# Convolution copies routed through DRAM in five transfers a piece, and the first worker's local attention woven with the tail of the second worker's scan

## What is computed

```python
# L0_attn: Mamba-2 on the GRU's output g; then x = x + branch + g
zxbcdt = g @ W_in
xBC = silu(causal depthwise convolution, 16 taps, of zxbcdt[..., 256:640] + conv_b)   # 384 channels
# y: the scan over 128 positions with the states B, C and dt
y = rmsnorm(y * silu(z)) @ W_out
t = y / sqrt(1 + y * y);  out = t @ W_nl + b_nl + g

# L0_cond2: attention to three neighbours and one conditioning key, 16 heads of 64
q, k = x @ WQ_w + WQ_b, x @ WK_w + WK_b;  ak, av = cond @ WK_w + WK_b, cond @ WV_w + WV_b
K = [ak, k[t-1], k[t], k[t+1]];  V = [av, k[t-1], k[t], k[t+1]]
att = softmax(q . K / 8) . V;  out = att @ WO_w + WO_b
```

## Time and profile before

| what | value |
|---|---|
| median of 3 executions (range) | 2227.7 us (2224.23 to 2228.19) |
| the profiled execution's own time | 2227.43 us |
| its span in the profile | 2225.7 us |
| mean granted TensorE clock | 0.951 of full speed |
| busy: PE / DVE / ACT / POOL | 1960.3 / 1593.2 / 1006.9 / 466.7 us |
| GRU ends, convolution and scan start | about 234 us |
| worker 0's / worker 1's Mamba ends | 606 / 649 us |
| attention ends | 1034 us |

### The profile page before, as it was taken

How to read it: one execution, slowest core, us unless ns; L and a number is a source line. 1 busy time by engine, 2 the same in 40 slices (tenths; PEclk the granted TensorE clock), 3 DMA queues, 4 the chain that set the end, 5 groups by cost and what they waited for, 6 DMA issues and landing times.

```text
span 2225.7 us, 63875 instructions
## 1 busy us (share of the span) xinstructions
PE 1960.3 (88%) x26197; PEld 1227.9 (55%) x26273; DVE 1593.2 (72%) x3661; ACT 1006.9 (45%) x2843; POOL 466.7 (21%) x816
## 2 busy tenths in 40 slices
PE   8989688888778989887899999967999789999998
PEld 5555233333353434434577767655666456677776
DVE  3444557777647787876988888726989578888887
ACT  3333347666622222122555555433554445555554
POOL 2221000000002343434012122254331111112100
PEclk9999789999969899997999999978999999999999
DMA  3000344332000000002211111016552211111111
GB/s 66 4 4 4 74 99 87 71 85 53 30 24 0 1 1 1 1 1 62 76 45 43 45 43 45 25 38 127 110 100 54 67 40 45 45 45 45 42 57 37
DMA packets 133228, 102.42 MB, mean 46 GB/s; under 512 B 23532, under 2 KB 114244, under 8 KB 131364
## 3 DMA queue, kind: packets, MB, share of 16 engines
q1 hardware_dynamic: 129352, 96.04, 17.8%
q10 hardware_dynamic: 3584, 2.30, 0.3%
HBM read 60.24 MB, written 11.82 MB: 32 GB/s over the span
## 4 chain that ended last, share of the span: by engine, by line
PE 47%; DVE 24%; ACT 12%; issue 9%; SPq 3%; DMA 2%; ACTq 1%; POOL 1%; another core or an unknown queue 0%; DVEq 0%; POOLq 0%
PE B L85 46%; DVE work L2251 4%; ACT catt L103 4%; DVE work L107 4%; DVE hr L2215 3%; DVE work L2259 3%; SPq L897 2%; ACT hr L103 2%; ACT ltc L103 2%; ACT work L103 2%; DVE work L1627 1%; DVE gzh L107 1%; ACT ghh L103 1%; ACTq L2538 1%; DVE lth L107 1%
## 5 line engine op out<-in xcount | busy, mean ns | idle before, releaser
L85 PE MATMUL B<-gr,wres 128*128 128x512 f32 x1248 | 352.9, 411 | 15.8 <-DVE work L2259 9.4
L103 ACT ACTIVATE work<-B 128x512 f32<-128x512 f32 (+6 forms) x462 | 236.3, 528 | 143.8 <-PE B L85 99.4
L2301 POOL COPY G<-lh 128x32 f32<-128x32 f32 x256 | 148.3, 579 | 679.9 <-DVE lh L107 679.9
L85 PEld LDWEIGHTS B<-gr,wres 128*128 128x128 f32 x1248 | 214.1, 189 | 82.6 <-DVE work L2259 26.8
L103 ACT ACTIVATE hr<-work 128x512 fp32r<-128x512 f32 x272 | 172.9, 636 | 147.8 <-DVE work L2259 77.8
L2215 DVE TENSOR_TENSOR hr<-work,hr 128x512 fp32r<-128x512 f32 x272 | 186.5, 686 | 8.1 <-ACT hr L103 6.6
L2251 DVE TENSOR_TENSOR work<-work 128x512 f32<-128x512 f32 x256 | 178.6, 698 | 14.7 <-ACT work L103 7.2
L85 PE MATMUL B<-hr,wres 128*128 128x512 f32 x624 | 178.0, 394 | 1.0 <-DVE hr L2215 1.0
L103 ACT ACTIVATE lth<-B 128x96 f32<-128x96 f32 (+1 forms) x512 | 86.7, 222 | 185.9 <-PE B L85 185.8
L85 PEld LDWEIGHTS B<-lh,lw 128*32 128x32 f32 x8128 | 88.5, 112 | 112.8 <-issue 58.6
L85 PE MATMUL B<-lh,lw 128*32 128x32 f32 x8128 | 116.7, 199 | 25.1 <-DVE lh L107 24.3
(11 more groups left out here) (270 smaller groups left out, 3850.2 us busy)
## 6 DMA issues: line engine op xcount, KB each, us to landing
work<-wdr SPq DMA_DIRECT2D x128, 256.0 KB, 3.1
spare<-work SPq DMA_DIRECT2D x288, 65.0 KB
scr<-catt SPq DMA_DIRECT2D x144, 64.0 KB, 2.8
spare<-spare SPq DMA_DIRECT2D x96, 65.0 KB
work<-scr SPq DMA_DIRECT2D x16, 384.0 KB
work<-scr SPq DMA_DIRECT2D x16, 192.0 KB
catt<-in_L_ffn_ew SPq DMA_DIRECT2D x24, 128.0 KB, 2.4
work<-scr SPq DMA_DIRECT2D x16, 128.0 KB
```

The source lines that it names most:

```text
L85: return e.matmul(out, lhsT, rhs, start=start, stop=stop, skip_group_check=True)
L103: return e.activation(out, in_, func, bias=bias, scale=scale)
L2301: e.tensor_copy(self.G[:, :, t], self.lh[:, t % 4, :]).then_inc(*inc("l.pool", "h", li, t))
```

## The change

Two parts. **Copies.** Each piece's padded tile is written once to a DRAM buffer `xdr[n % 4]` (295 KB) and read back by four DMAs, one per group g, each into 32 partitions by all 16 block-sequence pairs (266 KB). SP issues the write of piece n + 1 ahead of the reads of piece n. ACT may reuse `XP[n % 4]` once its write has landed (`conv.w`), not once the reads have. **Weave.** `cond2_*(0)` is chained after `cprep` in worker 0's lane and `cond2_*(1)` after `mamba_*(1)` in worker 1's; `Gak` and `cak` move to the free tile `spare` and are copied at the end of `cprep_act`; worker 0's padding is zeroed on POOL ahead of worker 1's last addition to X (`cond2_clear`); COND2_BEHIND = 14 turns replace the 22 on PE, ACT and DVE (POOL keeps 22); one yield of `cprep_dve` goes.

```diff
@@ -137,7 +137,7 @@
 EXPERTS = (("L0_ffn_kernel_gating_EDF", "L0_ffn_kernel_up_EDF", "L0_ffn_kernel_down_EFD"),
            ("L1_ffn_ew1", "L1_ffn_ew2", "L1_ffn_ew3"))
 NT = 12
-COND2_LAG = 22
+COND2_LAG, COND2_BEHIND = 22, 14
 MAMBA_DT_TURNS = 6
 MDT_BATCHES, MDT_TURNS = (slice(0, 8), slice(8, NB)), (12, 13)
 MAMBA_UNIT_TURNS = ((10, 1, 1, 1), (24, 1, 1, 1))
@@ -218,8 +218,8 @@
     def tensor(self, e):
         self.load_pe(e)
         weave(self.gru_pe(e), self.mprep_pe(e))
-        weave(self.conv_pe(e), (self.mdt_pe(e), 2), chain(self.mamba_pe(e, 0), self.cprep_pe(e)), self.mamba_pe(e, 1))
-        weave(self.cond2_pe(e, 0), self.cond2_pe(e, 1))
+        weave(self.conv_pe(e), (self.mdt_pe(e), 2), chain(self.mamba_pe(e, 0), self.cprep_pe(e), self.cond2_pe(e, 0)),
+              chain(self.mamba_pe(e, 1), self.cond2_pe(e, 1)))
         self.mix_pe(e, 0)
         self.attn_pe(e)
         self.mix_pe(e, 1)
@@ -227,9 +227,8 @@
     def scalar(self, e):
         self.load_act(e)
         weave(self.gru_act(e), self.mprep_act(e))
-        weave(self.conv_act(e), (self.mdt_act(e), 2), chain(self.mamba_act(e, 0), self.cprep_act(e)), self.mamba_act(e, 1))
-        self.cprep_end_act(e)
-        weave(self.cond2_act(e, 0), self.cond2_act(e, 1))
+        weave(self.conv_act(e), (self.mdt_act(e), 2), chain(self.mamba_act(e, 0), self.cprep_act(e), self.cond2_act(e, 0)),
+              chain(self.mamba_act(e, 1), self.cond2_act(e, 1)))
         self.mix_act(e, 0)
         self.attn_act(e)
         self.mix_act(e, 1)
@@ -237,8 +236,8 @@
     def vector(self, e):
         self.load_dve(e)
         weave(self.gru_dve(e), self.mprep_dve(e))
-        weave((self.mdt_dve(e), 2), chain(self.mamba_dve(e, 0), self.cprep_dve(e)), self.mamba_dve(e, 1), self.conv_dve(e))
-        weave(self.cond2_dve(e, 0), self.cond2_dve(e, 1))
+        weave((self.mdt_dve(e), 2), chain(self.mamba_dve(e, 0), self.cprep_dve(e), self.cond2_dve(e, 0)),
+              chain(self.mamba_dve(e, 1), self.cond2_dve(e, 1)), self.conv_dve(e))
         self.mix_dve(e, 0)
         self.attn_dve(e)
         self.mix_dve(e, 1)
@@ -609,6 +608,7 @@
         self.tap = self.area([self.work, 74 * 256 - 96 * NT], [128, 3 * NT, 32])
         w = [self.spare, 0]
         self.XR = [self.area(w, [128, 16, 127 + NT // 4]) for _ in range(2)]
+        self.xdr = [self.nc.dram_tensor(f"xdr{i}", [32, 16, 144], F32, kind="Internal").ap() for i in range(4)]
         w = [self.work, 0]
         ar = lambda *s, dt=F32: self.area(w, list(s), dt)
         self.cvb = [ar(128, 3, 512) for _ in range(4)]
@@ -820,7 +820,7 @@
             e.wait_ge(*at("conv.in", n))
             if n >= 4:
                 e.wait_ge(*at("conv.acc", n - 4))
-                e.wait_ge(*at(f"conv.r{n % 2}", n - 4))
+                e.wait_ge(*at(f"conv.w{n % 2}", n - 4))
             act(e, self.XP[n % 4][:, :, 16:144], BI[:].rearrange("p (b t) -> p b t", b=4), ACT.Copy).then_inc(
                 *inc("conv.x", n))
         inputs(0)
@@ -886,16 +886,25 @@
 
     def conv_sp(self, e):
 
+        at, dma = self.at, self.dma
+
+        def write(n):
+            e.wait_ge(*at("conv.x", n))
+            if n >= 4:
+                e.wait_ge(*at(f"conv.r{n % 2}", n - 4))
+            e.dma_start(self.xdr[n % 4].rearrange("p (j b) t -> j p (b t)", j=4), self.XP[n % 4][:]).then_inc(
+                *dma(f"conv.w{n % 2}", n))
+        e.wait_ge(*at("conv.pad"))
+        write(0)
         for n in range(24):
-            e.wait_ge(*self.at("conv.x", n))
+            if n < 23:
+                write(n + 1)
+            e.wait_ge(*at(f"conv.w{n % 2}", n))
             if n >= 2:
-                e.wait_ge(*self.at("conv.taps", n - 2))
-            else:
-                e.wait_ge(*self.at("conv.pad"))
+                e.wait_ge(*at("conv.taps", n - 2))
             for g in range(4):
-                for j in range(4):
-                    e.dma_start(self.XR[n % 2][32 * g:32 * g + 32, 4 * j:4 * j + 4, :],
-                                self.XP[n % 4][32 * j:32 * j + 32, :, 1 + NT // 4 * g:128 + NT // 4 * (g + 1)]).then_inc(*self.dma(f"conv.r{n % 2}", n))
+                e.dma_start(self.XR[n % 2][32 * g:32 * g + 32, :, :],
+                            self.xdr[n % 4][:, :, 1 + NT // 4 * g:128 + NT // 4 * (g + 1)]).then_inc(*dma(f"conv.r{n % 2}", n))
 
     def conv_pool(self, e):
         e.wait_ge(*self.at("xt", 7))
@@ -1198,8 +1207,10 @@
         ca = [self.catt, 0]
         ar = lambda *s, dt=F32: self.area(ca, list(s), dt)
         self.WQ, self.WK, self.WO = ar(128, 8, 128), ar(128, 8, 128), ar(128, 8, 128)
-        self.Gak = ar(128, NB, 16)
-        self.cak = ar(128, NB, 16)
+        ar(128, NB, 32)
+        s = [self.spare, 1024]
+        self.Gak = self.area(s, [128, NB, 16])
+        self.cak = self.area(s, [128, NB, 16])
         self.avo = ar(16, NB, 128)
         self.a0 = [ar(16, 512) for _ in range(2)]
         w = [self.work, 7680]
@@ -1261,6 +1272,9 @@
         self.mamba_first_end(e)
         for x in (self.akb, self.avb):
             e.memset(x, 0.0).then_inc(*self.inc("cprep.pool"))
+        e.wait_ge(*self.at("mw1.pe", "y", 11))
+        e.wait_ge(*self.at("cprep.pe", "akv"))
+        self.cond2_clear(e, 0)
 
     def cprep_pe(self, e):
 
@@ -1327,10 +1341,6 @@
         yield
         split(1)
         yield
-
-    def cprep_end_act(self, e):
-
-        self.mamba_end(e)
         for B, x, name in ((self.bank[0], self.Gak, "Gak"), (self.bank[1], self.cak, "cak")):
             e.wait_ge(*self.at("cprep.pe", name))
             act(e, x.rearrange("p b (c i) -> p c i b", c=8), B[:].rearrange("p (c i b) -> p c i b", c=8, i=2),
@@ -1358,7 +1368,6 @@
                 e.wait_ge(*at("cprep.act", "w", i, h))
                 e.tensor_tensor(d[1][:], W[:, 4 * h:4 * h + 4, :].rearrange("p c m -> p (c m)"), d[0][:].bitcast(F32),
                                 ALU.subtract).then_inc(*inc("cprep.dve", "w", i, h))
-            yield
             yield
 
     def cond2_ring(self, wk, r):
@@ -1389,7 +1398,7 @@
         m, pe, dve, a = self.cd[wk], f"cd{wk}.pe", f"cd{wk}.dve", f"cd{wk}.act"
         Bs = self.bank[3 * wk + 2]
         sT = m["pr"][0]
-        for _ in range(COND2_LAG * wk):
+        for _ in range(COND2_BEHIND * wk):
             yield
         xr = self.gr[wk]
         e.wait_ge(*at("cprep.act", "cak"))
@@ -1574,6 +1583,8 @@
                 if j == 0:
                     e.wait_ge(*at(pe, "q", i, c))
                     e.wait_ge(*at(a, "k", i, c))
+                if i + n == 0:
+                    e.wait_ge(*at("mw1.pe", "y", 15))
                 if n >= 6:
                     e.wait_ge(*at(pe, "s", i, (n - 6) // 3))
                 elif i and n == 0:
@@ -1633,17 +1644,22 @@
             yield
             yield
 
+    def cond2_clear(self, e, wk):
+
+        m = self.cd[wk]
+        e.memset(m["KP"][:, :, :, 0:1], 0.0)
+        e.memset(m["KP"][:, :, :, 129:130], 0.0).then_inc(*self.inc(f"cd{wk}.pool"))
+        e.memset(m["AT"], 0.0).then_inc(*self.inc(f"cd{wk}.pool", "zero"))
+
     def cond2_pool(self, e, wk):
         at, inc = self.at, self.inc
         m, pe, dve = self.cd[wk], f"cd{wk}.pe", f"cd{wk}.dve"
         KP, pr = m["KP"], m["pr"]
-        self.mamba_end(e)
         if wk:
+            self.mamba_end(e)
             e.wait_ge(*at("cprep.act", "cak"))
             e.wait_ge(*at("cprep.avo"))
-        e.memset(KP[:, :, :, 0:1], 0.0)
-        e.memset(KP[:, :, :, 129:130], 0.0).then_inc(*inc(f"cd{wk}.pool"))
-        e.memset(m["AT"], 0.0).then_inc(*inc(f"cd{wk}.pool", "zero"))
+            self.cond2_clear(e, 1)
         for _ in range(COND2_LAG * wk):
             yield
         for i in range(4):

```

## The result

| | median us | runs | lowest and highest | ratio to before, 95% interval |
|---|---|---|---|---|
| before | 2227.9 | 10 | 2221.7 to 2235.4 | |
| changed | 2240.7 | 10 | 2236.4 to 2248.0 | 1.0072 [1.0056, 1.0088] |

By the ratio the change made the kernel 16 us slower (12.5 to 19.6); the two medians lie 12.8 us apart. The forecast was 2216.5 us, with a range of 2208 to 2224. The profiled execution of the changed kernel took 2236.7 us, its span 2234.9.

What follows compares the result with a forecast made beforehand. PE bounds the kernel (busy 88%), so gains come where it idles: SP's issuing at the convolution's start and the scan-attention seam. 2227.4 - 7.9 (copies) - 3.0 (weave) = 2216.5 us, range 2208 to 2224.

Steps and rivals of the forecast that it cites:

- the price of the trip in part 1: Convolution start: from issuing the write of piece n + 1 to landing piece n, 1.36 MB at 215 GB/s, 8.4 us.
- 7.9 forecast: Gain of the copies at the convolution's start: 7.1 us by piece 5 plus 0.8 at piece 8.
- the write is narrow: Rival, copies: a quarter of the DMA engines carries the write, trip 10.2 us, sum 2222.4 us; chance 0.22.
- Each us of trip: Convolution start: three trips on the path, pieces 0, 3 and 5, so 3 us for each us of trip.
- The cover: Later convolution pieces: piece 7, the tightest found, stays covered by PE's work for trips up to 9.9 us.
- the round trip is slow: Rival, copies: serial trip slower than before; gain about gone at 11.8 us, 2261 us total at 15; chance 0.06.
- the late seam: Seam between scan and attention: worker 1's tail done at 659 without full PE clock, a gain of only 0.9 us.
- SP's added wait: Convolution start: reads of piece n wait behind ACT's copy of n + 1; piece 3 still gains only 0.5 us.
- Part 2, up to worker 1's split: Seam: worker 0's keys at 633.8 instead of 652.31, tail done at 657, worker 1's split at 669.9 instead of 672.85.
- The forecast waits: Seam: ACT waits a few us for POOL's padding before worker 1's split, and PE behind it.
- so the stage and all behind it shift together: Attention stage: engine order stays as before, so the seam's 3.0 us gain carries through to the end.
- C: Experiments' theory: the attention stage changes length by several us merely with where PE's clock falls and rises.

Runs made afterwards that it cites:

- 13: The kernel before, with one more copy of Gak and of cak on ACT ahead of worker 0's split: 2228.9 us, ratio 1.0013.
- 14: The kernel before, with two more copies each of Gak and cak on ACT ahead of worker 0's split: 2229.8 us, ratio 1.0009.
- run 4: The full change, with the reads of piece n issued ahead of the write of piece n + 1: 2224.1 us, ratio 0.9993.
- run 6: The copies through DRAM with four writes a piece, without the weave (seam as before the change): 2215.9 us, ratio 0.9955.
- 5: The full change with one wide write ordered 128 x 576 on both sides, channel reordering left out: 2213.0 us, ratio 0.9946.
- 7: The kernel before, with the copies of the first eight pieces shared between SP's and POOL's queues: 2204.3 us, ratio 0.9910.
- 8: The full change with four writes a piece, those of the first eight pieces on POOL's queue: 2215.0 us, ratio 0.9959.
- 11: The kernel before with the first eight pieces' copies on two queues, plus the weave of the change: 2205.8 us, ratio 0.9903.
- 2: The weave alone, with the 16 copies within SBUF a piece of the kernel before: 2226.5 us, ratio 1.0004.
- 12: The weave alone on the kernel before, measured and profiled a second time: 2227.5 us, ratio 1.0012.

## Why the prediction was wrong

| | trip us | start us | steady us | median us |
|---|---|---|---|---|
| before | | 129.28 | 241.79 | 2227.9 |
| changed, write on 4 engines | 12.0 | 134.35 | 250.64 | 2240.7 |
| one write on 16 | 8.6 | 121.77 | 240.18 | 2213.0 |
| one write on 8 | 11.1 to 11.5 | 131.36 | 242.89 | 2230.0 |
| one write on 2 | 14.1 to 14.5 | 149.35 | 267.45 | 2276.4 |
| four writes on 16 | 9.8 | 121.84 | 242.51 | 2219.2 |
| reads first, write on 4 | | 128.86 | 243.32 | 2224.1 |
| before, two queues | | 111.59 | 240.18 | 2204.3 |

**The step that failed** is the price of the trip in part 1: "6.3 us, and with 2.1 for the landing a trip takes 8.4 us". It spread the write over all engines. The runs showed a write on 4 of 16 engines and a trip of 12.0 us. Where the write is wide, the price of the trip holds: with one write on 16 engines a trip takes 8.6 us, and the start shrinks by 7.5 us against 7.9 forecast. That these two are so close is in part luck, since the waits stand at pieces 0, 2, 3 and 4 and not at 0, 3 and 5. The whole kernel is 12.3 us faster than before (2213.0 against 2225.3 beside it); the 10.9 forecast had 3.0 of them from the weave, which gave nothing. The rival "the write is narrow" had the right mechanism, but "I take 10.2" was 1.8 us short of the measured trip. Its working had the write and the queued reads, but not that the issues stretch behind a narrow write (reads of 4.9 us instead of 2.6); whether this makes up the 1.8 us was not tested. Its chance of 0.22 was too low as well: "the twelve other engines can go ahead with the reads" is no help, since PE waits for the last part of each read.

**Each us of trip** weighs more than the 3 us given. From 8.6 to 12.0 the start grew by 12.6 us, 3.7 for each us. The waits stand at pieces 0, 2, 3 and 4. Piece 2 was left out of the sum: its reads now stand behind ACT's copy of piece 3, while its copies before were there in time (270.84 was no DMA wait).

**The cover** of 9.9 us for later pieces holds below it: at 8.6 us the steady part has no wait. At 12 us pieces of the steady part wait 1.1 to 1.2 us (369.67, 412.30, 458.49, 501.09) and 0.2 (547.95), 4.75 us in all, and it is 8.9 us longer than before. The rest comes with a lower clock of PE. The mean granted clock in the steady part was 0.94 against 0.96 before. The weave alone has no wait for a piece there, a clock of 0.94 too, and a steady part of 244.8 us in both its profiles; in before and runs 13 and 14 it is 0.96 and 241.5 to 241.8 us, in four others 0.97 and 240.2 us. So this is not chance from run to run but differs from kernel to kernel. What lowers the clock was not isolated. The rival "the round trip is slow" had this mechanism, and put its break-even at a trip of 11.8 us; by the runs it lies between 9.8 us, where the kernel was 0.3 to 0.5% faster than before, and 11.3, where it was 0.2% slower. One bound of the forecast is also off in its own terms: a trip of 9.9 us with the late seam gives 2227.4 - 3.4 - 0.9 = 2223.1, not 2222.

**SP's added wait** was seen ("the new wait eats what the fewer issues give") but other orders of SP's issues weren't priced. With a narrow write the turned order is worth 16.6 us (run 4), of which the wait is an unknown part.

**Part 2, up to worker 1's split, was right** in its steps. The weave alone has worker 0's keys 28.7 us after worker 0's last addition (forecast 633.8 - 605.1 = 28.7), the end of the tail at 52.6 (51.9) and ACT's split for worker 1 at 64.7 (64.8; before 67.8): the 3.0 us are there. The forecast waits are there as well. In the changed kernel itself the same three are 27.4, 49.1 and 61.2 us: the split comes 6.5 us sooner than before, beyond the forecast's 4.1. Over the eleven profiles with the weave the split stands at 60.9 to 65.3. So the steps are right and their size moves. What failed is "so the stage and all behind it shift together". The profiles of before, of the weave alone and of four writes without the weave (run 6), from worker 1's first keys to the first matmuls on G:

```profile
675.56:1033.72 358.16, 310.97 (x1299) 145.66 (x1317) 275.25 (x456) 77.87 (x128) 146.13 (x117) 0.93 0.00 1
```

```profile
673.97:1035.70 361.73, 317.95 (x1317) 147.56 (x1317) 275.34 (x456) 77.83 (x128) 146.05 (x117) 0.92 0.00 1
```

```profile
667.09:1020.93 353.84, 309.50 (x1317) 143.20 (x1317) 275.13 (x456) 77.80 (x128) 146.02 (x117) 0.94 0.00 1
```

DVE and ACT do the same work in the same time in all three. PE's busy time follows its granted clock: 309.50 us at 0.94 and 317.95 at 0.92, for the same 1317 matmuls, and the stage is 7.9 us longer. (The profile of before lacks 18 matmul records, so its 310.97 us is too low to compare; the copies alone, with 1316 records and a stage of 358.14 us, have 314.98.) Over all profiles the stage is 353.8 to 355.4 us long at 0.94, 356.5 to 358.2 at 0.93, 358.1 to 363.2 at 0.92 and 361.1 to 362.2 at 0.91. The first keys of the stage, before and with the weave alone:

```profile
675.56 1.62 PE L85 MATMUL B<-gr,hr 128*128 128x512 f32 x6 [1.65 <-DVE gr L1566]
```

```profile
673.97 2.90 PE L85 MATMUL B<-gr,hr 128*128 128x512 f32 x6 [3.19 <-DVE gr L1565]
```

Six matmuls take 2.90 us, half clock, after an idle time of 3.19 us, where they took 1.62 after 1.65. This is not the whole of it: in three other profiles with the weave they ran at full clock after some 3.2 us, and the stage took 356.5, 357.4 and 363.2 us. With the weave the stage took 356.5 to 363.2 us in eleven profiles, 361 on average; without it 353.8 to 361.1 in seven, 358 on average. So its length does vary without the weave (C), yet it lies some 3 us higher with it. What decides where the clock falls inside the stage was not isolated and stays open.

How much of the seam's gain is given back differs too. The weave alone has worker 1's keys 4.3 us sooner and loses 3.6 in the stage and 3.0 in the steady part. The changed kernel has them 7.8 us sooner and loses 2.6, so in its one profile the weave kept 5.2 us. The times of whole executions decide: with against without the weave the ratios are 1.0004 and 1.0012 (alone), 1.0072 against 1.0068, 0.9970 against 0.9955, 0.9955 against 0.9959, and 0.9903 against 0.9910. These six pairs average +0.04%, where 3.0 us would be -0.13%. The weave is worth nothing that can be told; that PE's clock takes its gain back is what the profiles suggest, and no run held the clock still to prove it.

The profiled execution of the changed kernel (2236.7 us) is 20 us above the forecast of 2216.5: 13 at the start (5.1 lost instead of 7.9 gained) and 9 in the steady part, less 2 because seam and attention stage together gained 5.2 in this profile instead of 3.0. The median is another 4 us higher, which no profile accounts for.

## What to carry to other kernels

Fewer and larger transfers help only if each keeps all the DMA engines: look at how many pieces the outermost dimension of both sides has before counting bytes, and price a chain of write, landing and read by its slowest engine. Where a queue's issuing is the bound and the engines are half idle, a second queue gives more than a detour that saves issues: here 20 us with eight pieces shared. A gain at a seam ahead of a PE-bound stage is not yet a gain in the kernel; the stage behind must be looked at with its clock, in more than one profile.

## What the runs showed of the hardware

- A write whose sides are ordered 4 x 32 x 576 used a quarter of the engines: a DMA share of 0.26 at 101 to 104 GB/s. With 2 x 64 x 576 the tail of a trip showed 0.16 to 0.17 at 26 to 27 GB/s. The trip took 8.6, 11.3, 12.0 and 14.2 us with 128, 8, 4 and 2 as outermost dimension.
- Reads issued behind a narrow write are issued more slowly: the median of an issue was 1004 ns, behind the one wide write 626.
- POOL's queue issued the same copies at 0.54 us each (eight in 4.33), no slower than SP (0.60 at the median, eight in 5.50 while both issued), and both queues together moved 178 GB/s where one had moved 100.
- Two profiles of the weave alone had the distances at the seam and the attention stage equal to 0.11 us, though the scan began 6.9 us apart in them (234.91 and 241.80). Two profiles of the four writes with the weave had stages of 361.83 and 356.47 us, and of the four writes without it 353.84 and 355.35: such lengths repeat in some kernels and not in others.
- The mean granted clock of the steady part and its length went together in kernels without a wait for a piece there: 0.97 and 240.2 us (runs 5, 7, 8, 11), 0.96 and 241.5 to 241.8 (before, 13, 14), 0.94 and 244.8 (2, 12).
